# Two reciprocal roots joined into one of 86 columns, at another place in GpSimd's order

## What is computed

```python
h = tok(x)                                     # frames @ D.T, 128 columns
h = h + attn(layernorm(h))                     # softmax(x x^T) x, per clip
h = h + ffn(layernorm(h), Wq, ..., down, up)

def ffn(x, ...):                               # 8 heads, 64 keys a half
    q = layernorm(x @ Wq.T + bq) * ln_g + ln_b
    s0 = l2norm(q[..., :32]) @ l2norm(keys0).T     # s1 alike
    sc0, ix0 = top_k(s0, 16)                       # sc1, ix1 alike
    fs, pos = top_k(sc0[..., :, None] + sc1[..., None, :], 16)   # of 256 sums
    w = softmax(fs)
    fi = the sums' indices, ix0 + ix1, at pos
    return einsum(gelu(x . down[fi]) * w, up[fi])
```

## Time and profile before

| | us |
|---|---|
| median of 3 executions | 2027.36 |
| lowest, highest | 2024.80, 2029.87 |
| the profiled execution | 2031.43 |
| its span, first to last instruction | 2029.6 |
| DVE busy | 1919.0 (95%) |
| PE busy | 1632.5 (80%) |
| POOL busy | 1433.2 (71%) |
| ACT busy | 1232.0 (61%) |

### The profile page before, as it was taken

The page is one execution under the profiler, slowest core; times in us unless marked ns, Lnnn a source line. Parts: engine busy times, 40 slices in busy tenths (PEclk is TensorE's granted clock), DMA queues, the critical chain, the costliest instruction groups (busy, mean ns, idle before and its releaser), DMA issues.

```text
span 2029.6 us, 47236 instructions
## 1 busy us (share of the span) xinstructions
PE 1632.5 (80%) x11023; PEld 1169.5 (58%) x11023; DVE 1919.0 (95%) x15718; ACT 1232.0 (61%) x3883; POOL 1433.2 (71%) x2561
## 2 busy tenths in 40 slices
PE   5577888788888888888888788888878888986667
PEld 3235566566656655665666556656656565655456
DVE  2499999999999999999999999999999999999992
ACT  3346666666666666566556766656675665665554
POOL 2247777686777767777776777777687777767775
PEclk8877888888888787888888787888888888788765
DMA  1000000000000000000000000000000000000000
GB/s 44 7 10 4 19 7 13 13 7 19 7 19 9 13 13 6 19 7 19 7 6 22 6 19 7 19 7 7 19 9 20 7 19 7 6 13 9 7 6 11
DMA packets 46669, 24.87 MB, mean 12 GB/s; under 512 B 4827, under 2 KB 46116, under 8 KB 46390
## 3 DMA queue, kind: packets, MB, share of 16 engines
q1 hardware_dynamic: 46390, 21.85, 3.9%
HBM read 11.58 MB, written 10.26 MB: 11 GB/s over the span
## 4 chain that ended last, share of the span: by engine, by line
DVE 79%; PE 11%; ACT 5%; issue 4%; POOL 1%; SPq 1%; DMA 0%; DVEq 0%; ACTq 0%
DVE idx L1071 11%; DVE idx L1078 11%; DVE hrest L1065 10%; DVE alpha L1039 10%; DVE vals L1069 7%; DVE vals L1062 7%; DVE c L1109 5%; DVE crest L1103 5%; DVE top L1106 3%; DVE top L1100 3%; PE QB L526 2%; DVE beta L1044 2%; PE FB L418 1%; PE QB L514 1%; DVE lo L1033 1%
## 5 line engine op out<-in xcount | busy, mean ns | idle before, releaser
L914 POOL TENSOR_TENSOR bw<-beta,wp 128x1024 bf16<-128x1024 bf16 x240 | 505.2, 2135 | 347.3 <-issue 171.6
L526 PE MATMUL QB<-bw,alpha 128*128 128x48 bf16 x5120 | 554.5, 277 | 106.7 <-issue 101.1
L526 PEld LDWEIGHTS QB<-bw,alpha 128*128 128x128 bf16 x5120 | 521.0, 150 | 149.2 <-issue 139.4
L749 ACT ACTIVATE WD<-QB 32x96 f32<-32x96 f32 x1280 | 307.6, 240 | 84.5 <-PE QB L526 71.6
L1039 DVE TENSOR_SCALAR alpha<-hi 128x1024 bf16<-128x1024 bf16 x640 | 274.9, 502 | 0.0
L475 PE MATMUL SC<-WK,hidT 128*128 128x512 f32 x320 | 241.0, 846 | 12.6 <-issue 11.8
L1071 DVE FIND_INDEX8 idx<-vals,sraw 128x8 uint32<-128x64 f32 x1280 | 250.6, 218 | 0.0
L1078 DVE FIND_INDEX8 idx<-vals,hrest 128x8 uint32<-128x64 f32 x1280 | 250.6, 219 | 0.0
L1065 DVE MATCH_REPLACE8 hrest<-vals,sraw 128x64 f32<-128x64 f32 x1280 | 249.6, 207 | 0.0
L1062 DVE MAX8 vals<-sraw 128x8 f32<-128x64 f32 x1280 | 169.1, 207 | 14.1 <-ACT sraw L729 14.1
L1069 DVE MAX8 vals<-hrest 128x8 f32<-128x64 f32 x1280 | 166.6, 208 | 0.0
(11 more groups left out here) (206 smaller groups left out, 3583.3 us busy)
## 6 DMA issues: line engine op xcount, KB each, us to landing
res<-h_scratch SPq DMA_DIRECT2D x80, 64.0 KB, 1.9
xin<-in_x SPq DMA_DIRECT2D x32, 128.0 KB
h_scratch<-h2n SPq DMA_DIRECT2D x32, 128.0 KB
out<-ofin SPq DMA_DIRECT2D x64, 64.0 KB, 1.5
h_scratch<-h2n SPq DMA_DIRECT2D x32, 28.5 KB
out<-ofin SPq DMA_DIRECT2D x16, 57.0 KB
xin<-in_x SPq DMA_DIRECT2D x32, 28.0 KB
xin<-in_x SPq DMA_DIRECT2D x32, 0.2 KB
```

The lines of the kernel that those rows point to most:

```text
L526: last = mm(bank[:, 48 * u:48 * u + 48], alpha[:, buf, a, :, 8 * p + u], bwv[:, :, a, :, 8 * p + u], start=(a == 0), stop=(a == 1))
L749: last = A(WD[r, RING[(t - 4) % NT], :, 8 * p:8 * p + 8], blocks[r, :, :, g], ACT.Copy)
L914: last = tt(bw[:, buf, NY * i:NY * i + NY, :], beta[:, buf, :, :], wp[:, buf, i, :].unsqueeze(1).to_broadcast([128, NY, 256]), ALU.mult)
```

## The change

The norm root of pair k and the row root of pair k+1 share one set of buffers of 86 columns: `root_x`, `root_xh`, `root_y`, `root_a`; columns 0 to 79 are the norms', 80 to 85 the rows'. DVE makes the rows' mean square (`row_mean`) between the second maximum and the guesses, and then one xh and one y over 86 columns. POOL runs one Newton root over 86 columns at t = 0, part 3, ahead of bw. The one of 6 columns at (0, 2) stays for pair 0 alone, and the one of 80 at t = 1 is gone. vs reads the result in `root_y`. newton1 now counts both, 12 steps for pair 0's rows and 12 for each pair's joint root. Pair 15 has no next pair: its root goes over 86 columns as well.

```diff
-        c15 = sb("c15", [128, 80])
+        c15 = sb("c15", [128, 86])
...
-        sv = [sb(f"sv{i}", [128, 6]) for i in (1, 2)]
+        root_x, root_xh, root_y, root_a = (sb(f"root_{w}", [128, 86]) for w in ("x", "xh", "y", "a"))
+        sv = [root_x[:, 80:86], sb("sv2", [128, 6])]
...
+        n2, rn = root_x[:, 0:80], root_y[:, 0:80]
...
             def front(j, t, p):
-                if (t, p) == (0, 2):
-                    pool.wait_ge(s["seed1_full"], j + 1)
-                    newton(sy[0][:], sxh[0][:], sa[:, 0:6], c15[:, 0:6], s["newton1"], 12 * j)
+                if (t, p) == (0, 2) and j == 0:
+                    pool.wait_ge(s["seed1_full"], 1)
+                    newton(sy[0][:], sxh[0][:], sa[:, 0:6], c15[:, 0:6], s["newton1"], 0)
...
-                if p == 0 and t == 1 and exists(k, t, 0):
-                    pool.wait_ge(s["seed4_full"], k + 1)
-                    newton(y4[:], xh4[:], na[:], c15[:], s["rn_steps"], 12 * k, rn[:])
...
-                    pool.wait_ge(s["rn_steps"], 12 * kk + 12)
+                    pool.wait_ge(s["newton1"], 12 * kk + 24)
...
+                if p == 3 and t == 0 and exists(k, t, 0):
+                    pool.wait_ge(s["seed4_full"], k + 1)
+                    newton(root_y[:], root_xh[:], root_a[:], c15[:], s["newton1"], 12 * k + 12)
                 if p == 3 and exists(k, t, 3):
...
-                after(dve, s["rn_steps"], 12 * j)
+                dve.wait_ge(s["newton1"], 12 * j + 12)
...
+                if j + 1 < PAIRS:
+                    row_mean(0, j + 1)
+                    dve.wait_ge(s["sv1"], j + 2)
                 dve.wait_ge(s["n2_steps"], 2 * j + 2)
-                seed(n2[:], xh4[:], y4[:], s["seed4_full"])
+                after(dve, s["vs_full"], NT * j)
+                after(dve, s["xn_full"], 2 * j + 2)
+                seed(root_x[:], root_xh[:], root_y[:], s["seed4_full"])
...
                             norms(k)
-                            if k + 1 < PAIRS:
-                                row_seed(0, k + 1, s["seed1_full"])
```

More of the change, by code:

```diff
@@ L143, in build @@
         ss = [sb(f"ss{i}", [128, 6]) for i in (1, 2)]
-        sv = [sb(f"sv{i}", [128, 6]) for i in (1, 2)]
-        sxh = [sb(f"sxh{i}", [128, 6]) for i in (1, 2)]
-        sy = [sb(f"sy{i}", [128, 6]) for i in (1, 2)]
+        root_x, root_xh, root_y, root_a = (sb(f"root_{w}", [128, 86]) for w in ("x", "xh", "y", "a"))
+        sv = [root_x[:, 80:86], sb("sv2", [128, 6])]
+        sxh = [root_xh[:, 80:86], sb("sxh2", [128, 6])]
+        sy = [root_y[:, 80:86], sb("sy2", [128, 6])]
+        n2, rn = root_x[:, 0:80], root_y[:, 0:80]
         sa = sb("sa", [128, 40])
@@ L159, in build @@
         nw = sb("nw", [128, 80])
[L160 to L164, removed]
         sraw = sb("sraw", [128, 3, 1024])
@@ L241, in build @@
             inner_full gelu_full gl_full hcs_full scores_full sraw_full eb_full
-            rn_steps halves_full vs_full cs_full idxf_full ci_full c2_full zexp_full m_full wexp_full zs_full
+            halves_full vs_full cs_full idxf_full ci_full c2_full zexp_full m_full wexp_full zs_full
             rz_full wz_full y_full st_full w1_full rest1_full w2_full rest2_full w3_full his_full lo_full
@@ L771, in _, with newton @@
             tt = nc.gpsimd.tensor_tensor
-            def newton(y, xh, a, c, sem_, base, end=None):
+            def newton(y, xh, a, c, sem_, base):
                 i = 0
                 for r in range(3):
-                    for o, p0, p1, op in ((a, y, y, ALU.mult), (a, a, xh, ALU.mult), (a, a, c, ALU.add), (end if end is not None and r == 2 else y, y, a, ALU.mult)):
+                    for o, p0, p1, op in ((a, y, y, ALU.mult), (a, a, xh, ALU.mult), (a, a, c, ALU.add), (y, y, a, ALU.mult)):
                         if i:
@@ L975, in setup, with row_mean, row_seed @@
                                     ALU.mult).then_inc(s["kn_full"], 1)
-            def row_seed(i, j, done):
+            def row_mean(i, j):
                 dve.wait_ge((s["ss1_full"], s["ss2_full"])[i], 2 * j + 2)
                 V.tensor_scalar(sv[i][:], ss[i][:], 1.0 / D, 1e-5, ALU.mult, ALU.add).then_inc((s["sv1"], s["sv2"])[i], 1)
+            def row_seed(i, j, done):
+                row_mean(i, j)
                 dve.wait_ge((s["sv1"], s["sv2"])[i], j + 1)
```

## The result

The changed kernel takes 2031.98 us (median of 15 executions, 2029.33 to 2035.41), the kernel before 2025.60 (15 executions, 2023.85 to 2029.87): ratio 1.0028, 95% interval 1.0022 to 1.0035. It is slower by about 6 us, just under the 0.3% that the prediction had called the line; the forecast was 0.4 us less.

What follows compares the result with a forecast made beforehand. DVE, busy 1919 of 2029.6 us, was taken to bound the kernel. Terms of -3.9, -8.45 and +12.0 sum to -0.4 us, which on the median of 2027.4 gives 2027.0 us; own range 2022 to 2033, chance 0.57.

Steps and rivals of the forecast that it cites:

- Part 1: DVE's guesses: mean first, then two joined guesses of 86 columns; 0.26 us less a pair, 3.9 us less in all.
- Part 2: POOL's norm root leaves the second tile, so its collision with DVE's alpha compares goes: 17.5 us, of which 8.45 kept.
- What is late next: At sv of tile 2 DVE would wait for ACT's unmoved squares; 9.0 of the 17.5 us come back.
- rooms: How much earlier DVE can reach sv before waiting: eight pairs 0.5 to 0.6 us, three 0.95, three none.
- Part 3: POOL's root at the first tile grows to 86 columns and collides with DVE's compares: 0.8 us a pair, 12.0 us more.
- sign of being wrong in the main: First-tile collision under 0.4 or over 1.2 us a pair, or a wait held covered becoming the chain to bw.
- The sum: All terms together: -3.9 - 8.45 + 12.0 = -0.4 us, put on the median, giving 2027.0 us.
- (a): ACT's squares at tile 2 come along, so the second tile's gain stays whole: -9.4 us, 2018; chance 0.15.
- (b): POOL's wide root does not hold up DVE's compares at the first tile: -12 us, 2015; chance 0.08.
- (c): Slower: first-tile compares and root steps alternate without overlap, 1.55 us a pair, 23 us; sum +11, 2038; chance 0.15.
- the four: The rivals (a), (b), (c) and a fourth, that the change does nothing of the kind or cancels otherwise, chance 0.05.

Runs made afterwards that it cites:

- e1_guess: The kernel before with the joined guess alone, POOL keeping its two roots where they stood: 2021.58 us, ratio 0.9977.
- b0: The kernel before, unchanged, profiled a second time: 2026.99 us (span 2025.2).
- e3_relief: The kernel before with the norm root's twelve steps at tile 1 left out, products taking the first guess: 2023.63 us, ratio 0.9985.
- e2_wide: The kernel before with the row root at tile 0 widened to 86 columns, the norm root at tile 1 kept: 2036.28 us, ratio 1.0049.
- f_after: The changed kernel with the two guesses for v's root at tile 3 read straight from PSUM: 2015.70 us, ratio 0.9933 to the kernel before.

## Why the prediction was wrong

**Part 1** was right: 0.26 us a pair was said, 0.25 is seen in the changed kernel (4.81 against 5.06 us from the first of the two maxima, L1017 and L1018, to lo), and e1_guess measures 4.7 us for a term of 3.9.

**Part 2** was right in its first half: the collision at tile 1 went in all pairs, 17.5 us. One reading in it was wrong without harm: only the second compare ends with Ye. The first takes 0.65 us from 937.19 and ends at 937.84, 0.95 us before Ye does; it overlaps the end of Yw (936.25 to 937.56).

Its second half, **What is late next**, is the step that failed, in two ways. It put 9.0 us on the wait at sv of tile 2, and it named no other place.

The 9.0 us were worked out as if DVE came to sv 1.16 us earlier, though by the same sum tile 0 has by then cost 0.8 - 0.26 = 0.54 us. With the 0.62 us that are left, the prediction's own rooms give 8 x 0.07 + 3 x 0.62 = 2.4 us. The runs bear that out. Measured from a pair's first maximum, the last square is out after 54.2 us in b0, 54.3 in e3_relief and 54.3 in the changed kernel: the squares stay put, as was said. DVE is ready for sv after 54.7, 53.6 and 54.0 us (means of pairs 2 to 14). In e3_relief, where tile 0 costs nothing, DVE is 1.1 us early and the wait grew by the 8 us that were forecast. In the changed kernel it is 0.65 us early, and the view of waits shows little more than b0's 5.6 us in 3 waits:

```profile
DVE sv L977 <- ACT hid L600: 6.8, 12, 3.3
```

By the table tile 2 took back 0.19 us a pair, some 3 us. So this term alone would have left 6 us more of the gain than forecast.

The next place, tile 3, was never looked at: there DVE has two short instructions that can be held up by bw, whose start hangs on PE and ACT and does not come earlier when DVE does. DVE now arrives (v, ahead of xh) when bw has run for 2.7 us instead of 3.5 (means of pairs 2 to 14), and waits longer. The two guesses took 1.13 us a pair more, 16 us over 14 pairs, and tile 3 as a whole 1.21. Tile 4 gave back 0.38. In all, some 3 us of the 17.5 were kept and not 8.45. The first profile of the kernel before had shown the place, in the means of the two guesses (0.58 and 0.67 us for 0.17 us of work), and the prediction did not use these rows:

```profile
L929 DVE TENSOR_SCALAR y<-v 128x40 int32<-128x40 int32 x12 | 8.1, 671 | 0.0
...
L928 DVE TENSOR_SCALAR xh<-v 128x40 f32<-128x40 f32 x12 | 6.9, 576 | 0.0
```

It had even seen that kind of hold-up, at tile 1, and looked for it only where the change itself moved POOL's work.

**Part 3** was right: 0.8 us a pair was said, 0.67 measured (51.45 less 41.39 us over 15 pairs), 10 us in e2_wide for a term of 12. The root's start and end were hit within 0.2 us. That the late xns would be covered held: e2_wide shows no further cost. That it does not cost more in company was assumed, and there it is 16 us, of which 6 are open. The prediction's own sign of being wrong in the main, a cost at tile 0 under 0.4 or over 1.2 us, did not come; it watched the wrong term.

**The sum** with the sizes seen from profile to profile is, per pair, +0.43 (tile 0, with the guess in it), -1.14, +0.19, +1.21, -0.38 = +0.31 us, and 4.6 us in spans (2029.8 against 2025.2); the medians say 6.4.

**The rivals.** (a) and (b) were wrong in direction. (c) had the direction by another mechanism, and the one it named did not happen: a root step cost a compare 0.17 us (0.67 over four steps), not 0.36. What happened was none of the four. The profile of before was also not the usual one, which the prediction noticed (4 us above the median) and passed over; it hides nothing of the failed step, since both profiles have the guesses of tile 3 held up.

## What to carry to other kernels

When an engine at the limit gets time back in the middle of a loop, follow it through every later place of the loop where it meets another engine, not to the first one only: waits, and also instructions that are longer in the middle of another engine's work than alone. A row whose mean is several times that of its like is such a place already, and here it was worth more than the whole change: reading two small operands from PSUM instead of SBUF gave 9 us on the kernel before and 19 on the changed one. When several changes are summed, let each later room be met by what is left of the lead after the earlier costs. And a gain behind the last of the hold-ups found here did pay in full: eight steps less ahead of tile 4 gave 32 us.

## What the runs showed of the hardware

A tensor_scalar from SBUF to SBUF of 40 columns of 4 bytes took 0.17 us alone and far longer when one of POOL's 2.13 us instructions had begun: y (int32) up to 2.17 us, xh (fp32) up to 1.93. The same two with PSUM as their source took 0.18 to 0.20 us in all 16 pairs of f_after, bw or not. The Trainium skill, VectorE: DVE Perf Modes, section Mode 2×_2P, says that the mode which uses both read ports is there only for a source in SBUF. The trace agrees as far as it can: it does not name the mode, but shows that the PSUM form is not held up.

Between short instructions the two engines took turns at less than the full price: beside root steps of 0.37 us the compares (bf16) took 0.55 to 0.59 instead of 0.42, and the root's steps started 0.50 apart instead of 0.45. The Trainium skill, SBUF — State Buffer, section Who interferes with whom, has the loser block for the winner's whole instruction; the trace agrees for bw, where y, 0.17 us of work, takes 2.17 us and ends with bw's third instruction, and shows less than half of that for the root's steps.
